# Third norm of the attention stage: rows turned by a memory round trip and VectorE instead of TensorE

## The reference, cut to what matters

```python
x = x + 0.5 * ffn(layernorm(x))      # first
x = x + attn(layernorm(x))           # second
x = x + 0.5 * ffn(layernorm(x))      # third

# ffn(y): dots = softmax(y @ centroids.T / 0.1); hits = dots > 0.01
#         out = (y @ weight.T + bias) masked by any(hits, axis=1) and any(hits, axis=0)[assignments]
# attn(y): per token, 32 query heads and 8 key/value heads of 32; scores over the feature
#          axis d (32 x 32 per token), softmax, and the product with v
```

## Time and profile before

| what | value |
|---|---|
| median of 3 runs | 1257.59 us (1253.8 to 1264.04) |
| profiled execution, first to last instruction | 1253.4 us |
| TensorE busy | 1224.9 us (98%) |
| VectorE busy | 841.3 us (67%) |
| ScalarE, GpSimd busy | 411.3 us, 419.6 us (33% each) |

### The profile page before, as it was taken

The page is one execution under the profiler, slowest core; times in us unless marked ns, Lnnn a source line. Parts: engine busy times, 40 slices in busy tenths (PEclk is TensorE's granted clock), DMA queues, the critical chain, the costliest instruction groups (busy, mean ns, idle before and its releaser), DMA issues.

```text
span 1253.4 us, 21699 instructions
## 1 busy us (share of the span) xinstructions
PE 1224.9 (98%) x8552; PEld 1052.8 (84%) x8552; DVE 841.3 (67%) x1207; ACT 411.3 (33%) x590; POOL 419.6 (33%) x551
## 2 busy tenths in 40 slices
PE   6999999999998899999999999999999999999998
PEld 5778888888887788888888888888888888887886
DVE  5644355345452378878788787887878865279887
ACT  4313222322210134443444444444444443212120
POOL 1225544543423634323333333333332200040322
PEclk8999999999998999999999999999999999999999
DMA  7376776776663345555555555455555554116785
GB/s 260 101 210 184 231 199 201 198 223 176 168 179 117 110 124 155 156 135 163 156 139 157 141 158 162 133 160 139 152 160 133 148 142 162 67 51 236 275 302 193
DMA packets 318693, 208.53 MB, mean 166 GB/s; under 512 B 258304, under 2 KB 281344, under 8 KB 318592
## 3 DMA queue, kind: packets, MB, share of 16 engines
q1 hardware_dynamic: 303712, 187.74, 52.0%
q10 hardware_dynamic: 14880, 19.40, 4.5%
HBM read 118.49 MB, written 88.60 MB: 165 GB/s over the span
## 4 chain that ended last, share of the span: by engine, by line
PE 90%; DVE 3%; DMA 2%; ACT 1%; issue 1%; SPq 1%; POOL 1%; POOLq 0%; DVEq 0%; ACTq 0%
PE ps_b L269 13%; PE ps_b L271 13%; PE ps_b L270 13%; PE ps_a L269 11%; PE ps_a L271 10%; PE ps_a L270 10%; PE ps_t L276 6%; PE ps_s L1348 5%; PE ps_s L283 2%; PE ps_s L285 2%; PE ps_s L1398 2%; PE ps_s L290 1%; DMA y_scratch<-xa 1%; SPq L398 1%; DMA ya_tok<-y_scratch 1%
## 5 line engine op out<-in xcount | busy, mean ns | idle before, releaser
L269 PE MATMUL ps_a<-w_hi,odd_hi 128*128 128x512 f32 x464 | 186.4, 402 | 0.0
L271 PE MATMUL ps_a<-w_hi,odd_lo 128*128 128x512 f32 x464 | 182.1, 392 | 0.0
L270 PE MATMUL ps_a<-w_lo,odd_hi 128*128 128x512 f32 x464 | 181.6, 391 | 0.0
L269 PE MATMUL ps_b<-proj_hi,y_hi 128*128 128x256 f32 (+1 forms) x512 | 177.7, 347 | 0.0
L271 PE MATMUL ps_b<-proj_hi,y_lo 128*128 128x256 f32 (+1 forms) x512 | 172.7, 337 | 0.0
L270 PE MATMUL ps_b<-proj_lo,y_hi 128*128 128x256 f32 (+1 forms) x512 | 172.0, 336 | 0.0
L303 POOL TENSOR_TENSOR var_eps<-moments,eps 128x1 f32<-128x1 f32 x96 | 18.4, 191 | 406.2 <-DVE moments L299 406.2
L661 POOL TENSOR_TENSOR x_ring<-x_ring,f_tmp 128x1024 f32<-128x1024 f32 x32 | 77.0, 2405 | 163.6 <-DVE probs L1112 135.4
L962 DVE TENSOR_TENSOR f_out<-ps_b,bias_a 128x512 f32<-128x512 f32 x30 | 20.7, 689 | 147.9 <-PE ps_b L271 147.9
L607 POOL TENSOR_SCALAR f_out<-f_out,token_on 128x1024 f32<-128x1024 f32 x30 | 85.6, 2854 | 88.3 <-DVE f_out L962 88.0
L271 PEld LDWEIGHTS ps_b<-proj_hi,y_lo 128*128 128x128 f32 x512 | 97.1, 190 | 10.8
(11 more groups left out here) (188 smaller groups left out, 2731.5 us busy)
## 6 DMA issues: line engine op xcount, KB each, us to landing
xa<-in_L_attn_x SPq DMA_DIRECT2D x32, 512.0 KB, 5.2
f_tmp<-f_scratch SPq DMA_DIRECT2D x32, 512.0 KB, 4.4
x_ring<-in_L_attn_x SPq DMA_DIRECT2D x32, 512.0 KB, 3.3
f_scratch<-f_out SPq DMA_DIRECT2D x30, 512.0 KB, 4.0
x_scratch<-x_ring SPq DMA_DIRECT2D x30, 512.0 KB, 3.3
y_scratch<-xa SPq DMA_DIRECT2D x28, 512.0 KB, 3.7
ya_tok<-y_scratch SPq DMA_DIRECT2D x112, 128.0 KB, 3.2
late<-x_scratch SPq DMA_DIRECT2D x22, 512.0 KB, 6.9
```

The source lines that it names most:

```text
L269: pe.matmul(acc, hi[:, k, :], w_h[:, k, cols], start=(k == 0), stop=False)
L270: pe.matmul(acc, hi[:, k, :], w_l[:, k, cols], start=False, stop=False)
L271: last = pe.matmul(acc, lo[:, k, :], w_h[:, k, cols], start=False, stop=(k == KB - 1))
```

## The change

The third norm of tiles 0 to 29 is no longer turned by TensorE. ScalarE writes the normed rows into a buffer of its own, `y3_tok`, with its columns in the order (a k j) instead of (k a j). SP stores them to memory (512 KB), and later in the iteration loads them back (512 KB) into `y3_turn`, with 32 by 32 blocks in the turned place. One iteration later VectorE transposes within blocks in place, ScalarE copies the high part, and GpSimd subtracts for the low part, which VectorE did before from PSUM. The two copies go from a contiguous row into the operand's place with a stride of 4 elements. Tiles 30 and 31 are still turned by TensorE, after the loop. Because the operand is ready one iteration later, the half products and the logits of a pair are one iteration later: half products run from iteration 6 to 33, and two of them in iteration 34; pairs' logits come in even iterations instead of odd ones. `norm_third` no longer waits for the scores.

```diff
+            y3_tok, y3_turn = sb2("y3_tok", [P, EMB]), sb2("y3_turn", [P, EMB])
...
+        def by_block(tile):
+            return tile.rearrange("p k (i b) -> p b k i", b=T4)
...
+                def store_y3(t):
+                    sp.wait_ge(y3, t + 1)
+                    sp.dma_start(y3_d[t].rearrange("a p f -> p a f"), y3_tok[:, :]).then_inc(y3_stored, 16)
+
+                def load_y3(t):
+                    sp.wait_ge(y3_stored, 16 * (t + 1))
+                    wait(sp, lo3, t)
+                    sp.dma_start(y3_turn[:, :], y3_d[t].rearrange("a (i b) f -> (a i) (b f)", b=T4)).then_inc(y3_in, 16)
...
                     if 3 <= i < NT + 1:
                         load_x(i + 1)
+                    if 0 <= i - 4 < NT - 2:
+                        store_y3(i - 4)
...
                                      qkv_tok[:, 2 * HD:3 * HD].rearrange("p (s e) -> p s e", e=D)).then_inc(v_stored, 16)
+                    if 0 <= i - 4 < NT - 2:
+                        load_y3(i - 4)
...
+                def low_third(t):
+                    hi, lo = third_set(t)
+                    pool.wait_ge(hi3, t + 1)
+                    pool.tensor_tensor(by_block(lo), y3_turn[:, :].rearrange("p (b k i) -> p b k i", b=T4, k=KB),
+                                       by_block(hi.bitcast(F32)), ALU.subtract).then_inc(lo3, 1)
...
                     if i + 1 < NT:
                         mask_first(i + 1)
+                    if 0 <= i - 5 < NT - 2:
+                        low_third(i - 5)
+                    if i + 1 < NT:
                         add_first(i + 1)
...
-                def norm_third(t, i):
+                def norm_third(t):
                     act.wait_ge(norm3, t + 1)
-                    act.wait_ge(t2, min(i, NT))
-                    act.wait_ge(scores, min(i - 1, NT))
-                    wait(act, t3, t)
+                    wait(act, y3_stored, 16 * t)
+                    normed(act, y3_tok[:, :].rearrange("p (a k j) -> p k a j", a=T4, k=KB),
+                           x_ring[t % RING][:, :].rearrange("p (k a j) -> p k a j", a=T4, k=KB), 2, t).then_inc(y3, 1)
+
+                def high_third(t):
+                    act.wait_ge(turn3, t + 1)
...
+                    act.copy(by_block(third_set(t)[0]), y3_turn[:, :].rearrange("p (b k i) -> p b k i", b=T4, k=KB)
+                             ).then_inc(hi3, 1)
...
-                    if i >= 6 and i % 2 == 0:
-                        pair_soft_exp(act, NP + (i - 6) // 2)
+                    if i >= 7 and i % 2 == 1:
+                        pair_soft_exp(act, NP + (i - 7) // 2)
+                    if 0 <= i - 6 < len(HALVES):
+                        store_third(i - 6)
                     if i == NT + 2:
-                        norm_third(NT - 2, i)
-                    if 0 <= i - 5 < len(HALVES):
                         store_third(i - 5)
+                        norm_end(NT - 2)
                     if 0 <= i - 4 < NT - 2:
-                        norm_third(i - 4, i)
+                        norm_third(i - 4)
+                    if 0 <= i - 5 < NT - 2:
+                        high_third(i - 5)
...
+                def turn_third(t):
+                    dve.wait_ge(y3_in, 16 * (t + 1))
+                    dve.transpose(y3_turn[:, :], y3_turn[:, :]).then_inc(turn3, 1)
...
-                    if i >= 7 and i % 2 == 1:
-                        pair_soft_out(dve, 1, NP + (i - 7) // 2)
+                    if i >= 8 and i % 2 == 0:
+                        pair_soft_out(dve, 1, NP + (i - 8) // 2)
+                    if 0 <= i - 5 < NT - 2:
+                        turn_third(i - 5)
...
-                    if 0 <= i - 4 < NT - 1:
-                        low_third(i - 4)
...
-                    if 0 <= i - 5 < len(HALVES):
+                    if 0 <= i - 6 < len(HALVES):
+                        product_third(i - 6)
+                    if i == NT + 2:
                         product_third(i - 5)
...
-                    if 0 <= i - 4 < NT - 1:
-                        transpose_third(i - 4, i)
...
-                    if 0 <= i - 4 < NT - 2 and i % 2 == 1:
-                        u = NP + (i - 4) // 2
-                        pe.wait_ge(lo3, i - 3)
+                    if i >= 6 and i % 2 == 0:
+                        u = NP + (i - 6) // 2
+                        wait_third(pe, i - 5)
...
+                transpose_end(NT - 2)
                 product_kept(3)
-                transpose_third(LAST, NT + 2)
+                transpose_end(LAST)
...
-    nc = _bacc.Bacc("TRN2", target_bir_lowering=False, num_devices=1)
+    nc = _bacc.Bacc("TRN2", target_bir_lowering=False, num_devices=1, dynamic_dma_scratch_size=1024)
```

More of the change, by code:

```diff
@@ L186, in half, with wait_third @@
             return slice(h * HALF, (h + 1) * HALF)
+        def wait_third(eng, t):
+            if t < NT - 2:
+                eng.wait_ge(lo3, t + 1)
+            else:
+                eng.wait_ge(lo3_end, t - NT + 3)
         def wait(eng, semaphore, value):
@@ L831, in high_late, with norm_end, high_end @@
                     act.copy(late_set(v)[0], ps_t[:, :, :]).then_inc(hil, 1)
-                def norm_third(t, i):
+                def norm_third(t):
                     act.wait_ge(norm3, t + 1)
-                    act.wait_ge(t2, min(i, NT))
-                    act.wait_ge(scores, min(i - 1, NT))
-                    wait(act, t3, t)
+                    wait(act, y3_stored, 16 * t)
[3 more added lines that the diff above has]
+                    act.wait_ge(turn3, t + 1)
+                    if t < 2:
+                        act.wait_ge(pair_done, NP)
+                        for h in range(2):
+                            act.wait_ge(ffn1[h], NT - 1 + t)
+                    else:
+                        act.wait_ge(pair_done, NP + t // 2)
+                        if t % 2 == 0:
+                            act.wait_ge(ffn3, t)
+                    act.copy(by_block(third_set(t)[0]), y3_turn[:, :].rearrange("p (b k i) -> p b k i", b=T4, k=KB)
+                             ).then_inc(hi3, 1)
+                def norm_end(t):
+                    act.wait_ge(norm3, t + 1)
+                    act.wait_ge(t2, NT)
+                    act.wait_ge(scores, NT)
+                    wait(act, t3, t - NT + 2)
                     normed(act, y_tok[:, :], x_ring[t % RING][:, :], 2, t).then_inc(y3, 1)
-                def high_third(t):
-                    act.wait_ge(t3, t + 1)
+                def high_end(t):
+                    act.wait_ge(t3, t - NT + 3)
+                    act.wait_ge(ffn3, len(HALVES))
+                    act.wait_ge(pair_done, 2 * NP - 1)
                     act.copy(third_set(t)[0], ps_t[:, :, :]).then_inc(hi3, 1)
@@ L893, in _ @@
                         keep_third(1)
-                    if 0 <= i - 4 < NT - 2 and i % 2 == 1:
-                        copy_pair(NP + (i - 4) // 2)
-                norm_third(LAST, NT + 2)
+                    if i >= 6 and i % 2 == 0:
+                        copy_pair(NP + (i - 6) // 2)
+                high_end(NT - 2)
+                pair_soft_exp(act, 2 * NP - 2)
+                norm_end(LAST)
                 keep_third(3)
-                high_third(LAST)
+                high_end(LAST)
                 norm_late(1)
@@ L1073, in _ @@
                         low_again(i - 1 - NT)
-                    if i >= 6 and i % 2 == 0:
-                        pair_soft_in(dve, NP + (i - 6) // 2)
+                    if i >= 7 and i % 2 == 1:
+                        pair_soft_in(dve, NP + (i - 7) // 2)
                     if 0 <= i - 4 < NT - 1:
@@ L1298, in product_kept, with transpose_end @@
                     product(pe, ps_b[:, half(h)], hi, lo, w_hi, w_lo, half(h)).then_inc(ffnk, 1)
-                def transpose_third(t, i):
+                def transpose_end(t):
                     pe.wait_ge(y3, t + 1)
-                    pe.wait_ge(lo2, min(i, NT))
-                    wait(pe, loe, i - NT)
-                    wait(pe, lo3, t)
+                    pe.wait_ge(loe, 2)
+                    wait(pe, lo3_end, t - NT + 2)
                     transposes(pe, y_tok).then_inc(t3, 1)
@@ L1308, in transpose_again @@
                     pe.wait_ge(ye, e + 1)
-                    pe.wait_ge(lo3, NT - 3 + e)
+                    pe.wait_ge(lo2, NT)
+                    wait(pe, loe, e)
                     transposes(pe, f_tmp).then_inc(te, 1)
@@ L1382, in _ @@
                         wait(pe, lo2, i)
-                        wait(pe, lo3, i - 3)
                         if i == 0:
@@ L1400, in _ @@
                         last.then_inc(heads, 1)
-                    if 0 <= i - 4 < NT - 2 and i % 2 == 1:
-                        fold_pair(NP + (i - 4) // 2)
+                    if i >= 6 and i % 2 == 0:
+                        fold_pair(NP + (i - 6) // 2)
+                transpose_end(NT - 2)
                 product_kept(3)
-                transpose_third(LAST, NT + 2)
```

(3 more changed lines are left out.)

26 lines of the change are left out of this document (13 added, 13 removed).

## The result

The changed kernel takes 1289.14 us (median of 4 runs, 1286.91 to 1291.21), the kernel before beside it 1257.28. The ratio is 1.0253, with a 95% interval of 1.0221 to 1.0286: 2.5% slower, where I forecast 1241 us and a range up to 1257. The profiled execution spans 1289.2 us, 35.8 more than before.

A forecast was written before the change was run, and what follows sets the result against it. TensorE, busy 98% of the span, was taken as the bound. Transposes -25.2, head +4.9, tail +3, SP's queue +1 make -16.3 us: 1237.1 on the profiled execution, 1241 us on the median 4.2 above it; range 1233 to 1257.

The forecast's parts named there:

- SP's queue and memory: Two more issues and 1 MB per tile on SP's queue, hidden unless they delay q: 1 us charged for the stage.
- rival A: SP's queue: q and k's store lands some 1.4 us later behind the third norm's store; 12 us, 1252 us; chance 0.20.
- B: SP's queue: q and k's store waits out a whole 3.0 us landing every short iteration; 38 us, 1278; chance 0.07.
- The reserve: Short iterations: q_diag ends at scores + 16.8, next scores due at + 17.4; 0.6 us to spare, 1.45 before.
- TensorE: Attention stage: without the transposes, 25.2 us off; scores to scores 17.4 and 19.7 us instead of 18.29 and 20.58.
- VectorE, ScalarE, Pool: Moved work in the attention stage stays hidden: VectorE's total unchanged, high part 1.5 us, Pool's subtraction 3 us.
- Rival C: Copies too slow: high part at 2.65 us, or Pool late and blocking VectorE; 1252 us; chance 0.10.
- The turn's load: SP's load back of the third norm's rows, issued after the store of v: hidden unless it delays q.
- Head: Before tile 3's scores: no half product in iteration 5, so TensorE waits 4.9 us for q_diag, which nothing moves.
- Tail: Iteration 34: TensorE waits for the last pair's logits, 3 us (1 to 5); a late f3 store could add 2.
- the sum: All terms for the whole kernel: -25.2 + 4.9 + 3 + 1 = -16.3 us, giving 1237.1 on the profiled execution.

The follow-up runs named there:

- 4: Changed kernel with the third norm's store issued just behind the q and k store instead of ahead of it: 1256.0 us, ratio 0.9985.
- 9: Changed kernel with the x_ring load moved behind the q and k store, the third norm's store left ahead: 1257.4 us, ratio 1.0005.
- 1: Changed kernel with the third norm's store and load both cut from 1024 to 128 columns: 1247.6 us, ratio 0.9927.
- 2: Changed kernel with VectorE turning a third buffer filled once, so the turn doesn't wait for the load; both transfers still run: 1283.7 us, ratio 1.0208.
- 7: Kernel 4 with the last stored f3 product of the loop stored after the last third norm's norm and high part: 1246.2 us, ratio 0.9923.
- 8: Kernel 7 with ScalarE's and Pool's 16-byte-step access made dense, parts in the wrong order: 1243.7 us, ratio 0.9896.
- 10: Changed kernel with only the load back cut to 128 columns, the store in full at its place: 1286.6 us, ratio 1.0240.
- 12: Kernel 7 with the x_ring load also moved behind the q and k store, ahead of the third norm's store: 1257.5 us, ratio 1.0003.
- 11: Kernel before plus the two transfers, read by nobody, with the added store behind the q and k store: 1257.6 us, ratio 1.0013.
- 6: Changed kernel with the third norm's store issued from ScalarE's queue right behind its norm: 1270.6 us, ratio 1.0113.

## Why the prediction was wrong, and where it was right

**The step that failed** is "SP's queue and memory": "I charge 1 us in all for the stage, between 0 and 15 x 2.2". It took the landing of the earlier trace rows (3.0 us), which was read with one large transfer ahead, for a queue that now has two. I looked at the DMA engines between 709 and 712 us and found them idle, but that says how they are with one transfer, and the new store comes right behind the x_ring load. Measured: the landing rose by 1.4 us in the median and by up to 3.2; 4 and 9 put the price at 32 to 33 us. By the landing alone it is rival A (+ 1.4 us, chance 0.20), priced at 12 us. That the loss is larger has two more links of the same loop in it. These are means over the 14 short iterations from tile 3 on, in us:

| kernel | scores to q and k store | store to q_head | q_head to q_diag's start | q_diag's end after scores |
|---|---|---|---|---|
| 1, both thin | 8.45 | 3.08 | 3.84 | 17.1 |
| changed | 8.91 | 4.38 | 4.64 | 19.6 |

So q_diag is 2.6 us later, and the store's landing is only half of that (1.3). The landing of q_head is 0.8, and 0.5 is the store's later issue. That last part is not what decides: in 2 the store goes out at 8.48, and TensorE waits 24.9 us in the same iterations. The waits come to 2.1 us, near B's 2.4, in 12 of its 15 places, and half clock comes on top. So the size is B's, 11 us above its 1278, and B had 0.07; but B's way, the store waiting out a whole landing of 3.0 us, was seen in one tile only (6.2), and its number was met by another sum. The sign both rivals named, TensorE waiting for q_diag in every second iteration, is what the profile shows.

**The reserve** of 0.6 us in short iterations was right. That the same order costs 33.1 us here and 20.8 in the kernel before fits it: the edit took away slack that had covered this loop. No run changed the reserve alone, so this is argued.

**TensorE: right.** 17.4 and 19.7 us per iteration were forecast, and 7 shows 17.42 and 19.72 where nothing waits; over the 28 iterations from tile 3 its means are 17.9 and 19.9. The 25 us are real; in the changed kernel they are spent as waiting.

**VectorE, ScalarE, Pool: covered, with sizes off.** The high part takes 2.04 us, not 1.5; Pool's subtraction 2.97, as reckoned (3). Rival C would have had 11 us from the copies; 8 gives 2.5, not clear of noise. The Trainium skill (GPSIMD Engine Reference, Performance pitfalls for Q7 kernels) has reads in steps of over 8 bytes cost half as much again. Measured is 2.97 / 2.42 = 1.23, with one of the subtraction's two inputs and its output in such steps.

**The turn's load: hidden, or nearly, as reckoned,** though VectorE waits 48.1 us for it in all: 10 (thin) and 2 (no wait) recover 2.6 and 5.4 us, both near the noise.

**Head: 4.9 reckoned, 8.2 measured** (6.7 in 1), with half clock behind it. "Nothing in the change moves that" was wrong: even with thin transfers the inputs of tile 3's scores are there 53.6 us after tile 0's, not 51.6. A part of it is the x_ring load's, which isn't new: in 9 and 12, where that load goes behind the q and k store, the head's wait is 5.5 and 6.3 us, and for k_diag; in 4 and 7, where it stays ahead, it is 8.4 and 8.2.

**Tail: 3 reckoned, 5.3 + 0.5 and up to 3.4 of clock measured.** I had named "a late f3 store could add 2" and left it out; it was the case, and 7 takes 9.4 us out of the tail.

**The clock** had no term. That half clock followed some of TensorE's waits makes an idle microsecond dearer than a microsecond, and a forecast with a new wait in it should have carried that.

**Open.** Why single landings of over 4 us come in the fast orders too, in 1 to 5 of 32 tiles of kernels 1, 4, 7, 9, 11 and 12, and in 7 of 6 (3.9 at most in the kernel before); how far a single store of 512 KB must be ahead to cost nothing; why the head's inputs come 2 us later with thin transfers. 7's median lies 4.9 us above the forecast. In its profiled execution the way from tile 3 to tile 31 takes 1017.7 - 487.9 = 529.8 us, where the sum has 544.2 - 23.5 = 520.7. Of these 9.1 us, 1.9 are in the iteration behind the head, at half clock, and 4.2 around one late landing (4.8 us, from 582.2 on); the others are small pieces.

## What to carry to other kernels

Before adding a transfer, find the store or load whose landing sits in the loop that sets the rhythm, and count what is on the queue ahead of it, with its own reserve; put the new transfer right behind it in the queue, not right ahead of it. Then count again for the next link: in 12 two large transfers behind the store were two ahead of the load that follows, and cost 11 us. A landing time read where one large transfer runs ahead says nothing of two. When an edit shortens the bounding engine's iteration, it uses up slack of the other loops at once, so the cheap term to check is the smallest reserve, not the largest cost.

## What the runs showed of the hardware that was not expected

- A 512 KB load and a 512 KB store issued within 0.4 us, 2 to 3 us ahead of another store on the same queue, lengthen that store's landing from 3.0 to 4.4 us in the median (6.2 at most). The load alone, 2.4 us ahead, leaves the median at 3.0 (kernel 4), with a 512 KB store issued 0.4 us behind; so does the store alone, 5.4 us ahead (9). The load that follows the store is held too when two such transfers stand ahead of it: 4.7 against 3.8 us until its data is used (12 and 7).
- Half clock (0.50 granted) came with the head's wait of 8.2 us (10.2 us of it, wait included) and followed the waits of 2.18, 2.40, 2.61, 2.38 and 2.09 us before 552.7, 594.1, 675.3, 794.7 and 1034.1, for 3.4 us each. Waits of 2.08, 2.48, 2.64 and 2.83 us (before 635.3, 754.9, 954.0 and 994.7) were not followed by it, so their length doesn't tell the two apart.
- Steps of 16 bytes on fp32 cost ScalarE's copy 2.04 against 1.05 us and Pool's subtraction 2.97 against 2.42.
